# A new order on VectorE, ScalarE and GpSimd at the change of unit in a state-space mixer

## The reference

```python
proj = input_states @ in_proj_w.T
gate = proj[..., :INTER]                      # 8192 channels
xBC = silu(conv4(proj[..., INTER:INTER + CONV]) + conv_b)   # four taps along the tokens
hs, Bm, Cm = split(xBC)                       # 128 heads of 64, 8 groups of 128 states
scores = (Cc @ Bc) * Ldec * dt                # causal within a chunk
y_intra = scores @ xc
y_inter = (Cc * exp(cum)) @ prev              # the state carried from chunk to chunk
y = y_intra + y_inter + D * hs
g = y * silu(gate)
g = g * rsqrt(mean(g * g) + EPS) * norm_w     # the mean over one group of 1024 channels
return g @ out_w.T
```

## Time and profile before

| | us |
|---|---|
| median of 3 runs | 2132.67 |
| lowest, highest | 2129.69, 2134.03 |
| profiled execution, its own time | 2127.0 |
| its span | 2125.0 |
| mean granted clock of TensorE, of full speed | 0.979 |
| busy: TensorE matmuls, VectorE, ScalarE, GpSimd | 1984.3, 1671.7, 1441.9, 1283.2 |

### The profile page before, as it was taken

The page is one execution under the profiler, slowest core; times in us unless marked ns, Lnnn a source line. Parts: engine busy times, 40 slices in busy tenths (PEclk is TensorE's granted clock), DMA queues, the critical chain, the costliest instruction groups (busy, mean ns, idle before and its releaser), DMA issues.

```text
span 2125.0 us, 34073 instructions
## 1 busy us (share of the span) xinstructions
PE 1984.3 (93%) x11288; PEld 1533.7 (72%) x11288; DVE 1671.7 (79%) x3231; ACT 1441.9 (68%) x2755; POOL 1283.2 (60%) x1185
## 2 busy tenths in 40 slices
PE   8899997799999999999999999999999999999878
PEld 4666665587777777777777777777777777777665
DVE  4777665578897888888878887888788878888876
ACT  1566623677778777777787778787778787777721
POOL 4455230266777676767675767585667676766561
PEclk9999998899999999999999999999999999999989
DMA  4000010333223323232323232222222332222201
GB/s 169 2 0 0 0 56 5 95 113 104 76 78 101 114 65 97 88 112 68 109 74 116 64 105 99 85 85 89 95 89 81 94 104 90 80 90 80 85 29 40
DMA packets 125707, 166.04 MB, mean 78 GB/s; under 512 B 37777, under 2 KB 88977, under 8 KB 121330
## 3 DMA queue, kind: packets, MB, share of 16 engines
q1 hardware_dynamic: 125554, 164.11, 24.0%
HBM read 159.88 MB, written 4.20 MB: 77 GB/s over the span
## 4 chain that ended last, share of the span: by engine, by line
PE 39%; DVE 21%; ACT 19%; issue 6%; POOL 2%; SPq 0%; DMA 0%; ACTq 0%; POOLq 0%; DVEq 0%
DVE conv L807 11%; PE p_out L102 10%; PE p_mix L102 9%; PE p_gate_intra L102 7%; ACT wq_t L1773 4%; DVE w_out L1898 3%; PE p_gate_intra L1688 3%; ACT L1773 3%; PE p_inter_state L1664 3%; ACT L1783 3%; PE p_inter_state L1677 2%; ACT conv L785 2%; PE pM L102 2%; ACT x_and_gate L1783 1%; PE p_flip L1582 1%
## 5 line engine op out<-in xcount | busy, mean ns | idle before, releaser
L2108 POOL TENSOR_TENSOR wq_t<-wq_t,cb 128x1024 f32<-128x1024 f32 x128 | 316.4, 2472 | 224.2 <-ACT wq_t L1773 188.8
L102 PE MATMUL p_out<-w_out,yT 128*128 128x512 f32 x1536 | 386.7, 402 | 26.9 <-DVE attn L1936 13.8
L102 PEld LDWEIGHTS p_out<-w_out,yT 128*128 128x128 f32 x1536 | 295.1, 193 | 98.3 <-DVE yT L1918 17.3
L807 DVE SCALAR_TENSOR_TENSOR conv<-p_mix,unit_small,conv 128x511 f32<-128x511 f32 (+2 forms) x384 | 286.8, 747 | 98.7 <-ACT conv L785 87.2
L102 PE MATMUL p_gate_intra<-x_high,w_gate 128*128 128x512 f32 x1024 | 350.0, 403 | 5.9 <-POOL w_gate L2091 3.4
L102 PE MATMUL p_mix<-x_high,w_x 128*128 128x512 f32 x1024 | 351.4, 405 | 1.4 <-DVE x_low L1148 1.4
L1773 ACT ACTIVATE wq_t<-wq_t,minus_cum 128x128 f32<-128x128 f32 x1024 | 326.0, 390 | 1.4
L795 ACT ACTIVATE x_and_gate<-conv 128x512 f32<-128x512 f32 x128 | 80.8, 631 | 271.3 <-DVE conv L807 271.1
L102 PEld LDWEIGHTS p_gate_intra<-x_high,w_gate 128*128 128x128 f32 x1024 | 193.4, 189 | 44.6 <-POOL w_gate L2091 3.7
L102 PEld LDWEIGHTS p_mix<-x_high,w_x 128*128 128x128 f32 x1024 | 193.8, 189 | 39.8 <-DVE x_low L1148 1.8
L2149 POOL TENSOR_TENSOR x_to_state<-x_tokens,group_dt_end 128x512 f32<-128x512 f32 x96 | 120.9, 1259 | 156.9 <-ACT x_tokens L1730 156.9
(11 more groups left out here) (242 smaller groups left out, 4404.9 us busy)
## 6 DMA issues: line engine op xcount, KB each, us to landing
cum_all<-cum_rows SPq DMA_DIRECT2D x128, 512.0 KB, 3.8
exp_cum<-exp_rows SPq DMA_DIRECT2D x192, 128.0 KB, 3.2
w_staged<-in_w_gate SPq DMA_DIRECT2D x16, 1024.0 KB, 5.4
w_raw_tiles<-in_w_x SPq DMA_DIRECT2D x64, 256.0 KB, 3.0
w_staged<-in_w_out SPq DMA_DIRECT2D x16, 1024.0 KB, 4.9
w_raw_tiles<-in_w_bc SPq DMA_DIRECT2D x16, 256.0 KB, 5.4
x<-in_x SPq DMA_DIRECT2D x1, 2048.0 KB, 18.6
out<-x_and_gate SPq DMA_DIRECT2D x8, 256.0 KB, 2.0
```

The source lines that it names most:

```text
L102: last = pe.matmul(dst, left[a](k), right[b](k), start=k == 0 and n_ == 0, stop=stop and k == tiles - 1 and n_ == 2)
L807: m = dve.scalar_tensor_tensor(self.conv[:, par, back:], self.p_mix[:, bank, 0:SEQ - back], w[:, TAPS - 1 - back:TAPS - back], self.conv[: ...
L2108: pool.tensor_tensor(decay[:, k % 2], decay[:, k % 2], cb[:, c].unsqueeze(1).to_broadcast([P, UNIT_HEADS, P]), ALU.mult).then_inc(decay_do ...
```

## The change

On VectorE y's low part of steps 7 and 15 is made in those steps, behind `make_y` and ahead of the taps. `out_halves` of chunk 14 goes into step 15, ahead of `make_y`. In steps 0 and 8 (but not in the very first step) the order becomes: two of the four low parts of the output weights, the taps of the x tile, the new state, `make_y`, `mean_square` of the chunk before (which stood in steps 1 and 9), the taps of the second convolved tile (in step 0 alone), and the other two low parts. On ScalarE, step 7 makes all eight exponentials of step 8 ahead of `high_y`, steps 0 and 8 copy the next x out ahead of the second tile's activation, and steps 4 and 12 copy x out ahead of the second four exponentials. On GpSimd, steps 4 and 12 do the work on x, and in step 12 the inverse root, ahead of `decayed`.

```diff
--- before.py
+++ after.py
@@ -1772,7 +1772,7 @@
                         head = half * UNIT_HEADS + h
                         m = act.activation(decay[:, k % 2, h], decay[:, k % 2, h], ACT.Exp,
                                            bias=neg[:, s // STEPS % 2, c, head:head + 1])
-                    if hi == UNIT_HEADS:
+                    if lo < hi == UNIT_HEADS:
                         m.then_inc(exp_done, 1)
 
                 def silu_gate(s):
@@ -1829,19 +1829,21 @@
                                 out_high_part(g * 2 + half, half)
                             if half:
                                 keep_half(*before)
+                            if before:
+                                empty_x(g, k + 1)
                             for i, (e, _, index) in convs[1:]:
                                 channels_of(e, index, PLAN.conv_parity(k, e), g, k)
                             if not before:
                                 silu_gate(-1)
                                 silu_gate(s)
-                            empty_x(g, k + 1)
+                                empty_x(g, k + 1)
                             continue
 
                         decay_exps(s, k, 0, UNIT_HEADS // 2)
                         high_y(*before)
-                        decay_exps(s, k, UNIT_HEADS // 2)
                         if c == CPS:
                             empty_x(g, k)
+                        decay_exps(s, k, UNIT_HEADS // 2)
                         square_y(*before)
                         if s + AHEAD < TILES:
                             silu_gate(s)
@@ -1854,9 +1856,10 @@
                             if half and not last:
                                 group_exps(g + 1)
                             if not (last and half):
-                                decay_exps(s + 1, (k + 1) % STEPS, 0, UNIT_HEADS // 2)
+                                first_part = UNIT_HEADS // 2 if half else UNIT_HEADS
+                                decay_exps(s + 1, (k + 1) % STEPS, 0, first_part)
                                 high_y(g, k)
-                                decay_exps(s + 1, (k + 1) % STEPS, UNIT_HEADS // 2)
+                                decay_exps(s + 1, (k + 1) % STEPS, first_part)
                             if not half:
                                 keep_half(*before)
                             elif not last:
@@ -1890,9 +1893,9 @@
                 dve.memset(neg_half[:], -0.5).then_inc(const3, 1)
                 dve.memset(one[:], 1.0).then_inc(const3, 1)
 
-                def out_low_part(unit, half):
-
-                    for j in range(UT):
+                def out_low_part(unit, half, lo, hi):
+
+                    for j in range(lo, hi):
                         at_ = UT * (TAPS + 1) + j
                         dve.wait_ge(out_high, unit * UT + j + 1)
                         dve.scalar_tensor_tensor(wo[:, 1, j], staged[:, j], small[:, half, at_:at_ + 1],
@@ -1986,11 +1989,9 @@
                         events = PLAN.events(g, k, last)
                         before = None if first and k == 0 else (g if k else g - 1, (k - 1) % STEPS)
                         older = None if first and k < 2 else (g if k > 1 else g - 1, (k - 2) % STEPS)
-                        if c == 0 and before:
-                            y_low_part(*before)
-                        if older:
+                        if older and c != 1:
                             mean_square(*older)
-                        if older and older[1] >= CHUNKS:
+                        if older and older[1] >= CHUNKS and k:
                             out_halves(*older)
                         if c > 1 and not (last and k == STEPS - 1):
                             arguments(s + 1, (k + 1) % STEPS)
@@ -2001,7 +2002,7 @@
                             dve.tensor_tensor(cb[:, c], p_mix[:, bank, P:2 * P], causal[:], ALU.mult).then_inc(cb_done, 1)
                         if c < 2:
                             arguments(s + 1, k + 1)
-                        if c and before:
+                        if c:
                             y_low_part(*before)
                         if carries(c):
                             nc_ = n_carries(g, k)
@@ -2028,26 +2029,12 @@
                             front.bc_high_part(dve, g * 5 + 6, c - 1)
 
                         def taps_of(events):
-                            for i, (e, fill, index) in enumerate(events):
+                            for i, (e, fill, index) in events:
                                 if e[0] != "cb":
                                     front.run_taps(dve, e, index, PLAN.parity(k, i), PLAN.conv_parity(k, e),
                                                    1 - half if c >= CPS else half)
 
-                        if c == CHUNKS - 1:
-                            make_y(g, k)
-                            taps_of(events)
-                            if last and half:
-                                ahead_norm(k)
-                            continue
-                        if c == 0 and not (first and k == 0):
-                            out_low_part(g * 2 + half, half)
-                        taps_of(events)
-                        if 3 <= c < 3 + UT and not (last and half):
-
-                            front.x_high_part(dve, g * 5 + 4 + 3 * half + (c - 3) // 2, c - 3)
-                        if first and k == 0:
-                            out_low_part(0, 0)
-                        if feeds(c):
+                        def keep_state():
                             nf = n_feeds(g, k)
                             flat = state[:].rearrange("p h e -> p (h e)")
                             dve.wait_ge(st_done, nf + 1)
@@ -2056,6 +2043,35 @@
                                 dve.tensor_tensor(flat, p_state[:], flat, ALU.add).then_inc(state_done, 1)
                             else:
                                 dve.tensor_copy(flat, p_state[:]).then_inc(state_done, 1)
+
+                        convs = [(i, e) for i, e in enumerate(events) if e[0][0] != "cb"]
+                        if c == CHUNKS - 1:
+                            if half and not last:
+                                out_halves(*before)
+                            make_y(g, k)
+                            if not (last and half):
+                                y_low_part(g, k)
+                            taps_of(convs)
+                            if last and half:
+                                ahead_norm(k)
+                            continue
+                        if c == 0 and before:
+                            out_low_part(g * 2 + half, half, 0, UT // 2)
+                            taps_of(convs[:1])
+                            keep_state()
+                            make_y(g, k)
+                            mean_square(*before)
+                            taps_of(convs[1:])
+                            out_low_part(g * 2 + half, half, UT // 2, UT)
+                            continue
+                        taps_of(convs)
+                        if 3 <= c < 3 + UT and not (last and half):
+
+                            front.x_high_part(dve, g * 5 + 4 + 3 * half + (c - 3) // 2, c - 3)
+                        if c == 0:
+                            out_low_part(0, 0, 0, UT)
+                        if feeds(c):
+                            keep_state()
                         make_y(g, k)
                         if last and k >= 2 * CHUNKS - 4:
                             ahead_norm(k)
@@ -2156,7 +2172,7 @@
 
                         if k == 0:
                             dt_end(g)
-                        if c % CPS == 0:
+                        if c == 0:
                             decayed(g, k)
                         pool.wait_ge(flip_out, s + 1)
                         if feeds(c):
@@ -2164,7 +2180,7 @@
                         to_scores()
                         if not (first and k < 2) and older[1] >= CHUNKS:
                             inverse_rms(*older)
-                        if c % CPS:
+                        if c:
                             decayed(g, k)
                         if k == STEPS - 2 and not last:
                             end_logs(g + 1)
```

## The result

The changed kernel takes 2117.84 us (median of 4 runs, 2113.83 to 2119.76) beside 2132.44 us for the kernel before (2129.69 to 2134.03): a ratio of 0.9939, 95% interval 0.9927 to 0.9951. It is faster by 14.6 us, and the forecast had said 31.4. Its profiled execution took 2118.76 us with a span of 2116.9 us and a mean granted clock of 0.98. Against the profiled execution before (2127.0 and 2125.0) that is 8.1 us of span. From the first step's scores to the last's, the mixer gains 10.9 us; ahead of it and behind it, where the change does nothing, the profiled execution after was 1.8 and 1.0 us longer.

What follows compares the result with a forecast made beforehand. TensorE, busy 93% of the span, was taken as the bound: its computing plus stalls. Gains of 11.5 + 17.6 + 1.8 + 0.5 = 31.4 us from 2132.7 gave 2101 us, range 2087 to 2113.

Steps and rivals of the forecast that it cites:

- steps 15, 0, 1: Earlier output product in step 0 gains 2.3 us where the clock fell (four groups), 0.75 elsewhere (three): 11.5 us.
- steps 7, 8, 9: Stalls of 1.25 us in step 8 and 1.68 in step 9 go; 2.2 us gained eight times, 17.6 us.
- steps 4 and 12: Step 4's 0.7 us stall goes, step 5 waits 0.5: 0.25 us gained seven times, 1.8 us; step 12 nothing.
- last group: The last group's step 12 has the same wait as step 4; removing it gains 0.5 us.
- so nothing is late by this: Steps 15 and 0: x's taps end 1.4 us later, at 818.3, before ScalarE's activation starts at 818.5.
- fit into ScalarE's wait for y of 1.36 us: Step 7: all eight exponentials ahead of `high_y` cost nothing; low part done at 918.7, not 920.2.
- A loss of 0.5 each if more than one tenth of the lateness survives step 5: Step 4's lower bound; the upper was 0.75 us gained each if `skip_part`'s pieces hold together.
- its new stall: Step 1: output product waits about 1.75 us for y's low part of chunk 0 (released by `yT`).
- The other new stall: Step 1: x product waits about 0.9 us for its bank, released by the C channels' later taps.
- The gain without the clock: Steps 0 and 1: 0.75 us in each of the three groups where the clock had not fallen.
- The edit doesn't do what it says: Rival: y's low part in step 7 or 15 waits for a late high part, taps too; 2112 us, chance 0.03.
- More turns lost, and the clock still falls: Rival: step 1's second stall halves the clock, another GpSimd turn lost in step 0 or 1; 2107 to 2120, chance 0.27.

Runs made afterwards that it cites:

- the load ahead: Changed kernel plus a one-column Silu on ScalarE before its wait for the late x tile's taps, scratch column behind all else: 2108.50 us, ratio 0.9896.
- both out of the way: Changed kernel with the Silu table loaded before the wait and four exponentials on either side of y's high part in step 7: 2107.17 us, ratio 0.9888.
- the one move alone: Kernel before with only `out_halves` of chunk 14 moved from the start of step 0 into VectorE's wait in step 15: 2118.16 us, ratio 0.9950.
- the kernel with steps 4 and 12 alone: Kernel before with only x copied ahead of the last four exponentials and GpSimd's decayed scores behind x's products: 2130.29 us, ratio 0.9995.

## Why the prediction was wrong

The direction was right (0.95 for faster). The time and the range, 2087 to 2113, were not. By its own terms, with the differences of the two profiled executions, in us:

| term | forecast | measured |
|---|---|---|
| steps 15, 0, 1 | -11.5 | -8.0 (0 and 1: -7.3; 15: -0.7) |
| steps 7, 8, 9 | -17.6 | -4.0 (8: +5.3; 9: -7.7; 10: -1.7) |
| steps 4 and 12 | -1.8 | +2.4 (4 and 5: +5.2; 12 and 13: -2.8) |
| last group | -0.5 | -1.0 |
| other steps | 0 | -0.2 |
| mixer | -31.4 | -10.9 |

**The step that failed** is one sentence under steps 15, 0 and 1: "ScalarE's activation of them starts at 818.5 anyway (a table load before it), so nothing is late by this." I had the load in front of the activation, but took it for work that was already going on. It is work that begins when the taps end. Taps that end 1.4 us later move load, activation and flip with them. Under steps 7 to 9 I did not ask the question again, and a wait of 1.2 us stood there eight times (9.6 us; with the load ahead, 1.26 us of step 8 went). Of the forecast's 17.6 us for these steps, 4.0 came; with the load ahead 14.5 did, and 17.5 with the skip product in one instruction too. In steps 0 and 1 the load ahead gave nothing back, as VectorE's queue holds step 1 there. The Trainium skill, "ScalarE: Activation LUTs", section "Step-by-step: what each stage is for", says that the compiler has put the load right before the activation that needs it. The trace agrees: the load starts 0.08 us behind the taps. The page's cost of about 2.7 us, a drain included, isn't what this case shows: the load is 1.28 us, and the activation starts 0.01 us behind it.

**Eight exponentials "fit into ScalarE's wait for y of 1.36 us"** failed too, 0.7 us eight times (12.93 us for step 8 instead of 13.66). The two don't add: with both out of the way step 8 is 12.50 us. The wait was read from a kernel where ScalarE was on time. In the changed one it comes 1.0 us late, and the lateness is made in step 4, by the turns that I had forecast there.

**Steps 4 and 5.** The turns are as forecast: four to five microseconds for four pieces (5.08 us). The price of the edit within these steps was small, as forecast (0.25 us; 0.1 measured, on either kernel). What was wrong is what the edit stands on, and that I let it end in step 5, while its lag ran on to step 8. I took TensorE 0.75 us ahead and the other engines where they had been. "A loss of 0.5 each if more than one tenth of the lateness survives step 5" was the bound, and it was passed: +0.73. It was also the wrong lateness, since that which arrives from step 1 is the larger.

**Steps 0 and 1.** The mechanism was right. The clock no longer falls (6.3 us of 8.0), `skip_part` lasts over 4 us (4.37), step 1's output product has its new stall (1.49 for 1.75), VectorE's queue is full. The other new stall, 0.9 us ahead of step 1's x product, did not come (0.15 us): the first flip's 0.97 us stood ahead of it instead. The gain without the clock was sized too high, at 0.75 us a group; it is 0.14. Here the wait of 0.7 us for the high part, which I counted against the taps, had to be counted against the whole queue: with the low part between the taps these steps gained another 5.4 us.

**The rivals.** "The edit doesn't do what it says" named 2112 us and a chance of 0.03 for a low part that waits and the taps behind it. That is nearest to the cause that came, and it stood with the wrong price, for I gave it cover and had no table load in it. "More turns lost, and the clock still falls" covers the measured time but not its cause: the clock did not fall.

**What was not told apart:** the 0.4 us that step 13 gained and the 0.25 us of step 10. They are there in all edits of the changed kernel but not with the one move alone. Why the median gained more than the profiled executions (14.6 and 8.2 us) is argued, not shown: a kernel before whose clock falls in seven groups would be 5 us longer than one where it falls in four. The 44 other executions of that kernel on record fit: those with a mean granted clock of 0.974 to 0.976 took 2128.8 to 2134.0 us, those with 0.977 to 0.982 took 2123.5 to 2127.6, and the profiled one had 0.979.

## What to carry to other kernels

Find the engine that has no gap over several steps. A wait that is added to its queue costs its full length there (0.67 us a group here), and a wait taken from TensorE inside that stretch was worth nothing (the flip's, 0.97 us); work or waiting taken from the full queue counted. When an instruction on ScalarE is made late, look whether a table load stands behind the same wait, and pull it forward with one column of the same function. Try the parts of a change alone: here a single move of 0.68 us of work, made alone, gave as much as the whole change, mostly because it kept the clock up (6.3 of 8.8 us), and the other parts together added nothing that the times can show.

## What the runs showed of the hardware

- The clock. Step 0's output product ran at half clock for part of its time in 4 of 7 groups behind a stall of 1.96 us, and in 5 of 7 in the kernel with steps 4 and 12 alone, which has that stall too. In the changed kernel and the fifteen others, whose stalls in steps 0 and 1 are at most 1.5 us, it never did. In steps 13 to 15 of the last group it fell in all eighteen, beside stalls of 3.0 to 4.4 us.
- VectorE and GpSimd. Turns are taken by instruction: a single skip product, 0.69 us when free (step 8), lasted 2.62 us beside GpSimd's scores, and what was spared there came back as longer instructions on both engines (1.03 us became 1.50).
- An operand's place. With yT four bytes further on the output product was 0.04 us longer for twelve matmuls (2.95 to 2.96 us, not 2.91). Some small tensors moved with it, nothing in the profile explains it, and it was not tried with other tensors.
